# Feed-forward stage of an attention and feed-forward block: transposes of the maxima one step earlier, split of the next input in other steps

## The reference

```
z   = layernorm(x);  zq = round(z * 127/max|z|) / (127/max|z|)      # per row
h   = zq @ w1q.T                                                    # 512 -> 2048, w1q in {-1,0,1} * scale
h   = conv over rows, 3 taps per channel, + bias;  g = silu(h)
gq  = round(g * 127/max|g|) / (127/max|g|)                          # max over the 2048 channels of a row
x   = x + gq @ w2q.T                                                # 2048 -> 512
```

## Time and profile before

| | |
|---|---|
| median of 3 runs | 1976.48 us (1971.20 to 1978.28) |
| profiled execution, own time | 1974.42 us |
| its span | 1972.6 us |
| busy in the span: PE, DVE, ACT, POOL | 84%, 67%, 58%, 55% |
| granted clock of PE, mean | 0.936 |

### The profile page before, as it was taken

How to read it: one execution, slowest core, us unless ns; L and a number is a source line. 1 busy time by engine, 2 the same in 40 slices (tenths; PEclk the granted TensorE clock), 3 DMA queues, 4 the chain that set the end, 5 groups by cost and what they waited for, 6 DMA issues and landing times. The chain is left out here.

```text
span 1972.6 us, 31643 instructions
## 1 busy us (share of the span) xinstructions
PE 1650.0 (84%) x8834; PEld 714.7 (36%) x8834; DVE 1320.0 (67%) x1895; ACT 1137.3 (58%) x1851; POOL 1086.3 (55%) x755
## 2 busy tenths in 40 slices
PE   4888717798988974789999999999999984799998
PEld 2444313343433422333333333333333321344443
DVE  5988777888887786466666675757665653655653
ACT  3444338787777863356565656565655552666563
POOL 3455504777777882246565656465665652554542
PEclk9888859999998996799999999999999987899999
DMA  8121000000000002111010111111010101010101
GB/s 304 55 74 53 0 1 0 1 1 1 0 0 1 0 1 96 59 31 54 25 53 24 51 30 48 32 32 48 27 52 23 39 5 64 1 43 21 43 21 43
DMA packets 60442, 72.00 MB, mean 36 GB/s; under 512 B 14416, under 2 KB 40016, under 8 KB 59856
## 3 DMA queue, kind: packets, MB, share of 16 engines
q1 hardware_dynamic: 57520, 62.62, 10.1%
q10 hardware_dynamic: 2848, 8.52, 1.1%
HBM read 37.40 MB, written 8.39 MB: 23 GB/s over the span
## 5 line engine op out<-in xcount | busy, mean ns | idle before, releaser
L1283 DVE TENSOR_REDUCE s_mx<-bank 128x1 f32<-128x512 f32 x512 | 334.0, 675 | 245.2 <-PE bank L1388 242.6
L1209 ACT ACTIVATE s_E<-bank 128x512 f32<-128x512 f32 x512 | 293.3, 594 | 225.2 <-PE bank L1402 195.3
L1133 POOL TENSOR_TENSOR s_E<-s_E 128x1024 f32<-128x1024 f32 x128 | 300.0, 2355 | 154.5 <-PE bank L1410 128.8
L587 POOL TENSOR_TENSOR f_y<-f_y,f_t 128x511 f32<-128x511 f32 x128 | 167.3, 1309 | 108.2 <-DVE f_y L767 101.5
L1388 PE MATMUL bank<-s_KA,s_QA 96*128 96x512 f16 x512 | 193.7, 389 | 24.0 <-DVE s_mx L1283 14.8
L1402 PE MATMUL bank<-s_QA,s_KA 97*128 97x512 f16 x512 | 197.8, 388 | 12.0 <-ACT s_E L1209 8.0
L1126 POOL TENSOR_TENSOR s_qkl<-s_qkf,s_qkh 128x512 f16<-128x512 f32 x64 | 74.1, 1157 | 192.7 <-ACT s_qkh L1187 192.7
L1566 POOL TENSOR_TENSOR m_xl<-m_xf,m_xh 128x512 f16<-128x512 f32 x64 | 91.2, 1434 | 109.5 <-ACT m_xh L1609 109.5
L915 PE MATMUL bank<-f_w2q,w2raw 128*128 128x512 bf16 x512 | 132.2, 402 | 9.9 <-DVE w2raw L882 7.1
L1410 PE MATMUL bank<-s_E,s_V 128*32 128x512 f32 x1024 | 137.9, 611 | 2.8 <-ACT s_E L1209 2.8
L1287 DVE RECIPROCAL bank<-bank 128x128 f32<-128x128 f32 x128 | 121.3, 952 | 24.5 <-PE bank L1418 24.5
(11 more groups left out here) (235 smaller groups left out, 4047.9 us busy)
## 6 DMA issues: line engine op xcount, KB each, us to landing
X<-in_x SPq DMA_DIRECT2D x8, 1024.0 KB, 7.1
s_QA<-s_qkh SPq DMA_DIRECT2D x256, 32.0 KB, 1.8
s_KA<-s_qkh SPq DMA_DIRECT2D x256, 32.0 KB, 1.8
out_x<-X SPq DMA_DIRECT2D x8, 1024.0 KB, 4.2
a_cf<-in_ctx SPq DMA_DIRECT2D x8, 768.0 KB, 4.8
s_cf<-in_ctx SPq DMA_DIRECT2D x8, 768.0 KB, 4.5
w1raw<-in_w ACTq DMA_DIRECT2D x1, 4096.0 KB, 14.0
w2raw<-in_w ACTq DMA_DIRECT2D x1, 4096.0 KB, 29.2
```

The lines of the kernel that those rows point to most:

```text
L587: e.tensor_tensor(o, o, t[:, j % NTP, 0:S - 1], ALU.add).then_inc(s_c3.sem, 1)
L1133: e.tensor_tensor(into, into, other, ALU.add).then_inc(s_sum.sem, 1)
L1209: e.activation(E[:, SLOT[k] + h, :], SC[u % 2][:, :], ACT.Exp, scale=1.0 / float(np.sqrt(DH)))\
L1283: e.tensor_reduce(mx[:, q, h:h + 1], MX[q % 2][:, :], AX.X, ALU.max).then_inc(s_red.sem, 1)
```

## The change

Three edits, all in the order of the steps; no instruction is added, taken away or altered.

1. PE: `maxima(b - 1)` stands in step 4 instead of 5. Within step 4 it comes after `linear1` and after the two second products of that step.
2. ACT: the high halves of the four chunks are made in steps 10, 11, 11, 12 instead of 10, 11, 12, 13.
3. DVE: the low halves are made in steps 11, 11, 12, 12 instead of 10, 11, 11, 12, and the fourth statistics instruction in step 11 instead of 12.

```diff
@@ ACT, step @@
-                    if ahead and 10 <= j < 10 + KD:
-                        high(b + 1, 1 - odd, j - 10, zbank(j - 10))
+                    if ahead:
+                        for c in in_step(lambda c: (10, 11, 11, 12)[c] if c < KD else -1, j):
+                            high(b + 1, 1 - odd, c, zbank(c))
@@ DVE, step @@
-                        for c in in_step(lambda c: (10, 11, 11, 12)[c] if c < KD else -1, j):
+                        for c in in_step(lambda c: (11, 11, 12, 12)[c] if c < KD else -1, j):
                             low(b + 1, 1 - odd, c, zbank(c))
                     if ahead2:
-                        for q in in_step(lambda q: (7, 7, 10, 12)[q] if q < TT else -1, j):
+                        for q in in_step(lambda q: (7, 7, 10, 11)[q] if q < TT else -1, j):
                             stats(e, b + 2, q)
@@ PE, step @@
-                    if has_a and j == 5:
+                    if has_a and j == 4:
                         maxima(b - 1)
```

## The result

The changed kernel took 1960.29 us in the median of 7 runs (1957.38 to 1966.37), the kernel before 1978.28 us on the same chip (7 runs, 1971.20 to 1983.96): ratio 0.9914, 95% interval 0.9894 to 0.9935, 18.0 us faster by the medians. Forecast were 1946 us, 28.5 us faster, and a range of 1933 to 1964. The sign is right and the time lies in the wide range, 4 us from its upper end. The forecast's own bounds, 20 to 38 us faster, were missed: the gain is under two thirds of the sum, and nearer to the 15 us of rival (a), though not by its reason. The profiled execution took 1957.38 us, its span is 1955.6 us. One execution of a later kernel (diagonals on ACT in step 6) took 2422 us at a granted clock of 0.66 instead of 0.93, and its ratio leaves it out.

The account below looks back on a forecast made before the run. DVE was taken as the engine of the feed-forward loop, stalled 7.1 us in each 56 us period. Gains summed over the stage's batches to 28.5 us: 1974.4 - 28.5 = 1945.9, say 1946; range 1933 to 1964.

Parts of the forecast that it names:

- rival (a): Feed-forward stage: reordered halves work, the earlier maxima's gain is caught by POOL's or PE's run; 15 us, 1959; chance 0.18.
- The waits: DVE's stalls in a 56 us period: 3.57 us for the maxima's transposes, 3.5 for ACT's high halves, both to go.
- the term for clashes: More DVE tensor_scalar instructions meet a POOL instruction: 0.45 us lost a period, bounds 0.5 gained to 1.5 lost.
- rival (c): Slower: DVE's 18 tensor_scalar instructions a period clash with POOL, all at their slowest; 25 us slower, 1999; chance 0.03.
- The passage: POOL's long run, beginning with scaling, starts 3.0 us earlier: the narrower limit on the 3.57 us gained at DVE's scales.
- PE behind step 15: PE's 3.81 us idle before its first product of step 15 vanishes, with the slow matmuls behind it (0.61 instead of 0.38).
- lin1(j) needs taps(j-3): PE's first product of step j needs DVE's L767 from three steps earlier, as PE has three banks.
- b = 0: Feed-forward period without maxima: 1.8 us gained, an estimate, from the halves only.
- b = 1: Feed-forward period with only 1.78 us to give for the maxima and 3.5 for the halves: 3.3 us gained.
- b = 2 to 5: Four feed-forward periods like the one read, 4.5 us gained in each, 18.0 together.
- b = 6: Feed-forward period that waits 4.65 us instead of 3.57 for the maxima: 5.0 us gained.
- b = 7: Feed-forward period that waits 4.53 us for the maxima, but PE has no gap behind it: only 0.4 us passes.

Follow-up runs that it names:

- Edit 2 alone: Only the reordering of ACT's high halves and DVE's low halves and statistics, on the kernel before, maxima left in step 5: ratio 0.9971.
- both edits: The changed kernel itself: earlier maxima on PE, plus reordered halves on ACT and DVE, against the kernel before: 1960.29 us, ratio 0.9914.
- all three additions: Changed kernel plus POOL waiting for diagonals (step 3) and normalising (step 0), block 1's second product in step 15; against the kernel before: 0.9868.

## Why the prediction was right in sign and too large

- **The waits.** Right, both gone. The maxima earlier cost PE nothing visible: lin1(5) starts 1.41 us behind the start of the last reduction (L783, L782 before), as it did before (448.49 and 447.08; 458.66 and 457.25).
- **The step that failed is the term for clashes**, 0.45 us a period with bounds from -0.5 to 1.5. Ahead of it the sum had 4.95 us a full period, and 3.0 were measured, so the term came to 1.9, beyond its bound. In instructions it was 1.5 us at the diagonals, 1.4 at the roundings of steps 11 to 13 and 1.0 at normalising in three of four batches; part of the second lay in time in which DVE had waited. The row of L111 and L759 showed the spread. But the sum has no term for the diagonals at all, which leaves them at their 0.88 us in the one place where POOL stood idle, and it did not ask what POOL does in the time to which they move; by its timeline it was scaling and tapping there. They were also missing from the 18 instructions of rival (c), whose mechanism this is, at a smaller size than was needed to turn the sign.
- **The passage.** I held 3.0 of 3.57 to be what POOL's run lets through. No run tests this as such: with 2.14 coming in all of it passed, and with POOL held at the diagonals 2.4 passed. With the diagonals on ACT in step 6 some 4 us came in at taps(4) and 2.1 were left at taps(10), but there ACT had 1.3 us more to do, and PE's run was what held it.
- **Edit 2 alone**: 2.4 forecast, 2.27 measured at step 12. That nothing is lost between there and the scales was wrong by 1.3 us: 0.3 at the roundings of steps 12 and 13, and 1.0 at normalising, in batches of both kinds. With both edits normalising clashes in batches 2, 4 and 5, and in the odd ones DVE waits 0.8 to 1.0 us for PE.
- **PE behind step 15.** "lin1(j) needs taps(j-3)" does not hold at lin1(0) of an even batch: the banks turn with j + odd, so it needs taps(14), two steps back. So at the end of odd batches the idle and the slow matmuls moved and were not removed; at the end of batch 2 they were.
- **Term by term, forecast and measured**: b = 0 1.8 and 1.85; b = 1 3.3 and 1.5 (it gives back 1.8 between step 12 and the next batch); b = 2 to 5 4.5 each and 3.05, 2.81, 3.06, 3.11; b = 6 5.0 and 3.84; b = 7 0.4 and 0.5. Sum 28.5 and 19.7. Rival (c), clashes of DVE and POOL, had a chance of 0.03 as a case of its own; what came true of it was a share of the loss within the likeliest case.
- **What was luck.** The time lies in the range because the range was drawn wide enough to take in rival (a) at 1959. The bounds that the sum gave itself, 1936 to 1954, did not hold, and neither did the period of 51 to 52 us (it is 53) nor matmuls of 0.38 us all through it.

## What to carry to other kernels

A wait that is removed moves the instructions behind it into time in which the neighbour engine works: price each of them at its slow duration wherever POOL is busy in the new place, not at the one it has in the old. Read DVE's busy time per period beside its waits; when the waits fall and busy rises with equal counts, the gain has gone into contention. In this stage, with four engines busy within ten percent of each other, the two waits of 7.1 us a period were worth 3.0, and three small changes at the places that are late next, worth 0.7 to 1.8 us each, added up to 4.

## What the runs showed of the hardware

DVE's tensor_scalar instructions lengthen in steps: the four diagonals took 0.88, 1.38, 1.63, 2.40 or up to 2.67 us, four tiles of normalising in these batches 2.85, 3.84 or 4.82, according to which POOL instructions of 1.3 to 1.5 us lay beside them. The first two diagonals of batch 3 each ended 0.08 us behind the end of a POOL instruction. The Trainium skill ("SBUF — State Buffer", "SBUF: two separate sides") states an exclusive lock on the shared port pair, held for a whole instruction. The trace agrees with it: in these ends, and in the 1.38 us that the diagonals take with POOL's tap held back.

The untouched softmax stage differs between executions by more than such edits bring. From the first to the last exponential it took 803.2 us before (at 827.0 to 1630.2), 805.8 with both edits, 808.6 in their second profile, 811.4 with the diagonals on ACT in step 4 and 801.7 with all three additions; the records of granted clock in that stretch hold 10.2, 17.1, 30.7, 33.7 and 3.4 us at the lower of PE's two levels. Other stretches with unchanged code vary too: what lies ahead of the first taps took 300.9 us before and 297.1 after, and between 297.1 and 302.7 in all twelve profiles. So the fall of the profiled span, 17.0 us where the stage gained 19.7, is a sum of several such differences: 3.8 us less ahead of the stage, 2.6 more in the exponentials, and 3.8 more in the stretches between the stage and the exponentials and behind them. Whether the changed stage causes a part of what follows it stays open.
